# The spread stage of a graph kernel: edge pairs loaded two steps ahead into two buffers per quarter

## The reference

```python
# layer 0: attention over edges
out_i = softplus(concat(x[i], edge_attr) @ W).reshape(-1, 4, 64)
out_j = softplus(concat(x[j], edge_attr) @ W).reshape(-1, 4, 64)
alpha = softplus((concat(out_i, out_j) * att).sum(-1))      # then batch norm, softplus, segment softmax
x = layernorm(x + segment_sum(out_j * alpha, i).mean(heads) + bias)
# layer 1: two graph convolutions with symmetric norm and self loops
h = D @ (A + I) @ D @ (x @ W1) + b1                         # D = deg ** -0.5, A[d, s] = number of edges s -> d
h = D @ (A + I) @ D @ (h @ W2) + b2
x = layernorm(x + relu(h))
```

## Time and profile before

| | us |
|---|---|
| median of 3 runs | 6508.17 |
| the runs | 6492.07 to 6529.35 |
| the profiled execution, its own time | 6569.77 |
| its span, first to last instruction | 6568.1 |
| mean granted TensorE clock, share of full | 0.876 |

### The profile page before, as it was taken

How to read it: one execution, slowest core, us unless ns; L and a number is a source line. 1 busy time by engine, 2 the same in 40 slices (tenths; PEclk the granted TensorE clock), 3 DMA queues, 4 the chain that set the end, 5 groups by cost and what they waited for, 6 DMA issues and landing times. The chain is left out here.

```text
span 6568.1 us, 161934 instructions
## 1 busy us (share of the span) xinstructions
PE 4909.4 (75%) x32887; PEld 3154.3 (48%) x32888; DVE 4742.2 (72%) x21938; ACT 4010.7 (61%) x10577; POOL 3842.7 (59%) x5381
## 2 busy tenths in 40 slices
PE   1466676776767666674999999999948888886699
PEld 0234444444444344442555555555525556554699
DVE  6566666666666666664999999999986767777333
ACT  4344555555555555554999999989967777776100
POOL 1366666666666666565666666666637777776000
PEclk8577777777778888777999999999979999998799
DMA  8755555555555455555444444444417777775698
GB/s 227 232 180 180 188 188 182 186 185 186 189 174 179 167 172 178 168 177 153 104 103 104 103 105 105 103 103 104 103 40 218 216 216 224 215 212 176 247 360 345
DMA packets 1161941, 1148.62 MB, mean 175 GB/s; under 512 B 516532, under 2 KB 1023523, under 8 KB 1142980
## 3 DMA queue, kind: packets, MB, share of 16 engines
q1 hardware_dynamic: 1033656, 743.67, 40.2%
q0 software_dynamic: 88560, 319.28, 13.0%
q10 hardware_dynamic: 39580, 84.01, 3.4%
HBM read 716.98 MB, written 429.60 MB: 175 GB/s over the span
## 5 line engine op out<-in xcount | busy, mean ns | idle before, releaser
L914 POOL DMA_INDIRECT rows<-rowS,idx x1616 | 1732.5, 1072 | 1006.7 <-issue 469.7
L1185 PE MATMUL psa<-one_c,one_s 128*128 128x392 bf16 x2352 | 641.3, 393 | 654.8 <-DVE one_s L996 414.9
L2425 PE MATMUL psm<-msg,onem 128*128 128x260 f32 x3648 | 915.8, 394 | 212.7 <-issue 180.5
L988 DVE TENSOR_TENSOR one_c<-ioc,pairS 128x1176 bf16<-128x1176 f16 x784 | 599.4, 765 | 603.8 <-remote 340.4
L1699 DVE CUSTOM_DVE_ANT_1 junk<-bufh,attb 128x128 bf16<-128x128 f32 x3648 | 973.7, 301 | 0.0
L2346 POOL TENSOR_TENSOR msg<-oj,heads 128x512 f32<-128x512 f32 x760 | 796.9, 1072 | 215.3 <-DMA oj<-rows 179.0
L2425 PEld LDWEIGHTS psm<-msg,onem 128*128 128x128 f32 x3648 | 649.9, 190 | 478.2 <-issue 402.0
L1078 ACT ACTIVATE lgS<-preS 128x1024 f32<-128x1024 f32 x404 | 413.2, 1023 | 729.6 <-remote 375.4
L1659 POOL TENSOR_SCALAR one<-io128b,side 128x128 bf16<-128x128 bf16 x912 | 738.9, 810 | 63.5 <-DMA side<-rows 40.1
L1782 PE MATMUL pre<-P3h,oneT 128*128 x5472 | 757.0, 275 | 0.0
L1694 DVE CUSTOM_DVE_ANT_0 junk<-bufh,attb 128x64 bf16<-128x64 f32 x3648 | 742.1, 238 | 10.2 <-ACT bufh L1742 6.4
(11 more groups left out here) (306 smaller groups left out, 9238.3 us busy)
## 6 DMA issues: line engine op xcount, KB each, us to landing
oj<-rows SPq DMA_DIRECT2D x912, 256.0 KB
bufh<-rows SPq DMA_DIRECT2D x912, 128.0 KB, 2.5
adj<-adj SPq DMA_DIRECT2D x70, 1568.0 KB, 9.9
adj<-cnts ACTq DMA_DIRECT2D x49, 1568.0 KB
side<-rows SPq DMA_DIRECT2D x912, 68.0 KB, 2.3
eaS<-in_edge_attr_dram SPq DMA_DIRECT2D x201, 256.0 KB
low<-dlow SPq DMA_DIRECT2D x202, 252.0 KB
adj_early<-adj SPq DMA_DIRECT2D x28, 1568.0 KB, 8.4
```

Of the source, the lines that this page charges most:

```text
L914: eng.indirect_dma_start(out=m["rows"][h], out_offset=bass.IndirectOffsetOnAxis(ap=idx[s][:, k:k + 1], axis=0), in_=rows[s][:, k, :], in_o ...
L988: eng.tensor_tensor(one_c[r][:, :, :].rearrange("p k (a w) -> p k a w", w=WIDE), m["ioc"][:, q, None, :].rearrange("p k (a w) -> p k a w", ...
L1185: mm = eng.matmul(psa[r][:, 0:z.GC], one_s[r][:, k, :], one_c[r][:, k, :], start=(k == 0), stop=(k == GT - 1))
L2425: mm = eng.matmul(psm[j][:, 0:C + H], one[q][:, k, :], msg[q][:, k, :], start=(k == 0), stop=(k == UT - 1))
```

## The change

Each quarter gets two pair buffers, chosen by s % 2, with a semaphore each. SP loads the pairs of step t+2 where it loaded those of step t+1, and ahead of the loop it loads the pairs of steps 0 and 1. The wait before a load asks for `lanes` of step t as before, since the buffer that step t+2 takes is the one that step t used. `columns` counts the landings of its buffer by `turns(b, s)`, which is 2b + s // 2.

```diff
-        pair = [sb(ctx, f"pairS{q}", [P, GT, 2, WIDE], fp16) for q in range(GQ)]
+        pair = [[sb(ctx, f"pairS{q}{j}", [P, GT, 2, WIDE], fp16) for j in range(2)] for q in range(GQ)]
...
-        pair_in, cols_made, built, copied = ([sem(ctx, f"{n}{q}") for q in range(GQ)] for n in (
-            "pair_in", "cols_made", "built", "copied"))
+        cols_made, built, copied = ([sem(ctx, f"{n}{q}") for q in range(GQ)] for n in ("cols_made", "built", "copied"))
+        pair_in = [[sem(ctx, f"pair_in{q}{j}") for j in range(2)] for q in range(GQ)]
...
             def load_pairs(b, s, q):
                 t = step(b, s)
                 e = eng.value_load(m["startS"][0:1, span(t * GQ + q, 1)], min_val=0, max_val=NG * P * K)
-                wait(eng, cols_made[q], t)
-                eng.dma_start(pair[q][:, :, :, :].rearrange("p k n w -> p (k n w)"),
+                wait(eng, cols_made[q], t - 1)
+                eng.dma_start(pair[q][s % 2][:, :, :, :].rearrange("p k n w -> p (k n w)"),
                               m["pairs"][bass.ds(e, GT * P), :].rearrange("(p k) c -> p (k c)", k=GT))\
-                   .then_inc(pair_in[q], 16)
+                   .then_inc(pair_in[q][s % 2], 16)
 
             def body(b, s):
-                near, two = later(b, s, 1), later(b, s, 2)
+                two = later(b, s, 2)
                 if exists(*two):
                     load_ea(*two)
                     load_low(*two)
-                more = dense(near[0])
+                more = dense(two[0])
                 if more:
-                    load_pairs(*near, 0)
-                    load_pairs(*near, 1)
+                    load_pairs(*two, 0)
+                    load_pairs(*two, 1)
                 if exists(*two):
                     load_window(*two)
                 if more:
-                    load_pairs(*near, 2)
-                    load_pairs(*near, 3)
+                    load_pairs(*two, 2)
+                    load_pairs(*two, 3)
...
-            for q in range(GQ):
-                load_pairs(0, 0, q)
+            for s in range(2):
+                for q in range(GQ):
+                    load_pairs(0, s, q)
...
-                eng.wait_ge(pair_in[q], (t + 1) * 16)
+                eng.wait_ge(pair_in[q][s % 2], (turns(b, s) + 1) * 16)
```

More of the change, by code:

```diff
@@ L989, in columns @@
                                   m["ioc"][:, q, None, :].rearrange("p k (a w) -> p k a w", w=WIDE).to_broadcast(shape),
-                                  pair[q][:, :, 1, None, :].to_broadcast(shape), ALU.is_equal)
+                                  pair[q][s % 2][:, :, 1, None, :].to_broadcast(shape), ALU.is_equal)
             def lanes(b, s, q):
@@ L997, in lanes @@
                                   m["io128b"][:, None, :].rearrange("p k (a w) -> p k a w", w=WIDE).to_broadcast(shape),
-                                  pair[q][:, :, 0, None, :].to_broadcast(shape), ALU.is_equal).then_inc(cols_made[q], 1)
+                                  pair[q][s % 2][:, :, 0, None, :].to_broadcast(shape), ALU.is_equal).then_inc(cols_made[q], 1)
             def adj(b, s, q):
```

## The result

The changed kernel took 6549.37 us in the median of 4 runs (6542.57 to 6556.0), the kernel before 6501.04 us in the median of its 4 (6492.07 to 6529.35). The ratio is 1.006, with a 95% interval of 1.0036 to 1.0084. I had forecast 6493 us, in a range of 6448 to 6522: the change costs time where I had it gain a little. Two later comparisons on other chips gave 1.0049 [1.0032, 1.0067] and 1.0032 [1.0019, 1.0044]. The ratios are those on record, with their intervals; they are not the quotients of the medians printed beside them, from which they differ by up to 0.0016.

What follows compares the result with a forecast made beforehand. It found no engine full and took the stage as a chain of waits between engines that each run in order. The terms summed to −15 us, from the 6508 us median to 6493 us, range 6448 to 6522.

Steps and rivals of the forecast that it cites:

- The pair waits go: DVE before `columns`: waits for pairs, 88.4 us over the stage, fall to under 10 us.
- SP's lateness stays: SP at the block's end: q = 0 pairs still issued 2 to 3 us behind `load_ea`, eleven behind the last pairs.
- The cover that I had named: Stage start: four more pair loads delay `load_ea` by at most 4.3 us, hidden because DVE needs the low part later.
- Buffers, semaphores and the wait value cost nothing: Four more buffers and semaphores, and DVE's register work for the new wait value: cost 0.
- My slower rival: DVE's pair waits: computing each wait value costs 1.5 us per block, 74 us in all, giving 6567 us; chance 0.10.
- `psr` is late next: DVE's wait for PE's rank counts grows from 2.5 toward 3.8 us per block, leaving a gain of 15 us.
- the 6 us of the comparison: Stage halves with and without fills: 25 blocks with fills would gain 0.25 us each, 6 us.
- the 28 us of the single block: PE in one block: `adj` of q = 0 could start at most 1.4 us earlier, 28 us for 20 waits.
- the wait for `psr` took everything: Rival at DVE's wait for rank counts: it takes the whole gain, 6508 us, no change; chance 0.22.
- The comparison of the two halves: Stage blocks: 53.75 us each with fills, 53.50 us later with few pair waits, so pair waits do not set the pace.
- my forecast for this view: Block stores: every 53.0 to 53.6 us in the first half, still every 53.5 us in the second.
- The unnamed waits were pairs too: Rival before `columns`: the 340.4 us of "remote" waits also go, some 343 us gained in all, 6165 us; chance 0.02.

Runs made afterwards that it cites:

- buffers_only: Changed kernel with two buffers and semaphores per quarter and the new wait count, but all pairs loaded one step ahead; 6553.54 us, 0.9986 of the kernel before.
- after_again: The changed kernel timed once more, unedited, against the kernel before on the same chip; 6590.73 us, ratio 1.0049.
- after_third: The changed kernel timed a third time, unedited, against the kernel before on another chip; 6587.60 us, ratio 1.0032.
- q0_only: Changed kernel with only quarter 0 loaded two steps ahead, quarters 1 to 3 one step ahead; 6582.51 us, 1.0035 of the kernel before.
- the first question: Whether buffers and semaphores or the loads cost time: copies of both kernels and two partial versions, timed on a chip where the kernel before took 6557.84 us.
- gate_after2: Changed kernel, POOL's half 0 scatters at s = 0 held until PE made the next step's rank counts; 6559.12 us, 0.9994 of the kernel before.
- both exchanges: `add_up` of half 0 put ahead of the next step's `columns`: in the kernel before 6686.87 us, 1.0187; in the changed kernel 6697.06 us, 1.0193.
- gate_before2: Kernel before, with only the wait of POOL's half 0 scatters at s = 0 for PE's next rank counts; 6587.63 us, 1.0024 of the kernel before.
- the gate at s = 2: Changed kernel with the scatter gate at s = 2 instead of s = 0; 0.9971 and 0.9949 of the kernel before, both on 46-us chips.
- the gate together with the early `add_up`, addup_gate_before: Kernel before with `add_up` of half 0 ahead of `columns` and the scatter gate at s = 0; 6137.43 us, 0.9926, on a 46-us chip.
- the 1.9%: Loss from putting `add_up` of half 0 ahead of `columns` on a 54-us chip; 1.0187 in the kernel before, 1.0193 in the changed kernel.
- gate_after: Changed kernel, POOL's half 0 scatters at s = 0 held until PE made the next step's rank counts; 6146.62 us, 0.9953, on a 46-us chip.
- gate_before: Kernel before, with only the wait of POOL's half 0 scatters at s = 0 for PE's next rank counts; 6178.62 us, 0.9988, on a 46-us chip.
- the exchange alone: Kernel before with `add_up` of half 0 ahead of the next step's `columns`; 0.9932 on a 46-us chip, 1.0187 on a 54-us chip.
- before_again: The kernel before, unedited, timed against itself; 6556.47 us, ratio 0.9996.
- addup_first_after: Changed kernel with `add_up` of half 0 ahead of the next step's `columns`; 6697.06 us, 1.0193 of the kernel before.

## Why the prediction was wrong

**The pair waits go: right.** They fall from 80.3 to 1.8 us in the stretch of the earlier trace rows. For the whole stage I had said under 10.

**SP's lateness stays: right.** Over the 25 places behind a block's fills the first pair load follows `load_ea` by 3.6 us in the mean and the last pair load by 9.1 us (3.2 and 10.0 before). One of them:

```profile
1043.81 2.86 SPq L1445 DMA_DIRECT2D rows<-fill  x2
1047.29 0.36 SPq L844 DMA_DIRECT2D eaS<-in_edge_attr_dram  x1
...
1050.50 2.16 SPq L864 DMA_DIRECT2D pairS<-pairs  x2
```

At the stage's start `load_ea` of step 2 goes out at 300.78 us, 5.66 us later than before. The first pair load was already 0.58 us later (291.42 against 290.84), so the four more loads took 5.1 us where I had allowed 4.3. The cover that I had named holds all the same, for DVE has no wait before its use of step 2's low part at 308.61. SP's queue there and DVE's timeline:

```profile
300.78 0.37 SPq L844 DMA_DIRECT2D eaS<-in_edge_attr_dram  x1
```

```profile
308.12 0.57 DVE L940 TENSOR_TENSOR ohr<-io,hi_src 128x400 bf16<-128x400 bf16 x1
308.61 0.48 DVE L950 TENSOR_SCALAR ohT<-low,wsc 126x1024 bf16<-126x1024 bf16 x1
```

**Buffers, semaphores and the wait value cost nothing: right,** by 0.9986 for buffers_only. The instructions in question even fell, from 225 of 45 to 50 ns to

```profile
L985 DVEq FUSED_REGOPS  x45: 57/57/65, 342.6 to 2820.9; - x45
```

My slower rival, with its chance of 0.10, had the right sign for the wrong reason; nothing of its mechanism is there.

**`psr` is late next: right in the place, wrong in size and sign.** The term was "between the 6 us of the comparison and the 28 us of the single block", a gain of 15 us. The wait before L968 in the first half grew from 2.5 to 4.8 us per block (101.7 us over 21 blocks), where I had expected 3.8. The runs show not a gain but a loss, 20 to 40 us by the ratios. The step that failed is the one under the term: I took the time at which PE's counts are ready as given, so that the worst that could happen on this path was that the wait for `psr` took everything and the change gave nothing. I said what SP's queue would do and what DVE would wait for next, and did not ask what DVE releases earlier. It is `add_up` of half 0, and behind it the scatters on POOL. The waits of POOL showed it before the change: 246.5 us of waiting for DVE's `add_up`, the largest of its named waits in the stage. In its place the runs showed that with the new loads the scatters at s = 0 start 1.7 us earlier and the counts for s = 1 are ready 0.8 us later, and that a gate on these scatters brings the ratio from 1.0032 to 0.9994.

**The comparison of the two halves** showed that blocks without pair waits were no shorter, and that was a sound warning; but it compares two halves of one kernel and could not show a loss. The stores of the changed kernel, as the earlier trace rows:

```profile
L1112 ACTq DMA_DIRECT2D adj<-cnts x22: 338/338/361, 510.6 to 1631.6; - x22
...
L1112 ACTq DMA_DIRECT2D adj<-cnts x24: 338/339/365, 1688.9 to 2921.2; - x24
```

That is 1121.0 / 21 = 53.4 us and 1232.3 / 23 = 53.6 us, against 53.75 and 53.50. It is inside my forecast for this view, and it misled: in after_again, after_third and q0_only a block takes 54.5, 54.8 and 54.8 us over the whole stage. One profile of each kernel can't carry a difference of half a microsecond a block.

**The unnamed waits were pairs too: refuted** on 54-us chips, "remote" before `columns` stays at 361.2 against 340.4 us. The rule of the Trainium skill that the prediction weighed there ("Perfetto Trace Analysis", Optimization Strategy: a repeating gap can mean too few buffers) says what can be; for the pair buffers these runs do not bear it out: they were added and the gap kept 493.9 of its 603.8 us. Other buffers were not tried.

What stays open: by what way the early scatters make the count late, and how that costs a block its time. The trace shows PE's own rows over early and its consumers waiting. Timeline of the changed kernel in one bad block, PE, then DVE, then POOL:

```profile
728.92 0.81 PE L1157 MATMUL psr<-ohr,onesb 128*128 128x400 bf16 x5
730.09 0.29 PE L1157 MATMUL psr<-ohr,onesb 128*128 128x150 bf16 x3 [0.36 <-issue]
...
734.49 2.66 PE L1169 MATMUL preS<-W2d,eaT 64*128 64x256 f32 x5 [0.84 <-issue]
```

```profile
731.61 0.16 DVE L966 COPY rowS<-ends 128x16 f32 x1
738.97 0.57 DVE L968 TENSOR_TENSOR ranks<-psr,base 128x400 f32<-128x400 f32 x1 [7.20 <-remote]
```

```profile
731.36 0.96 POOL L915 DMA_INDIRECT rows<-rowS,idx  x1 [0.30 <-issue]
...
736.42 0.96 POOL L915 DMA_INDIRECT rows<-rowS,idx  x1 [0.30 <-issue]
740.21 0.95 POOL L915 DMA_INDIRECT rows<-rowS,idx  x1 [2.83 <-PE preS L1175]
```

The last rank matmul ends at 730.38 by the record, and DVE may go on only at 738.97, while POOL sends one scatter after another. ACT, which waits for the `adj` matmuls behind them (the last recorded to end at 732.82), goes on at 739.02 too, after 7.61 us without work. Whether the scatters' transfers, POOL's own work for them or something between PE and its supply of instructions is what meets, no run tells.

There is a rival that no run tests. The granted clock goes with the loss: on the chip of the first question the runs of the kernel before have a mean of 0.881, those of after_again 0.878 and of q0_only 0.879; on the chip of after_third it is 0.881 for before, 0.878 for after_third, 0.883 for gate_after2 and 0.873 for both exchanges. Among the runs of the kernel before on these two chips 0.001 less clock goes with 2 to 4 us more time, only loosely, so 0.003 would be 6 to 12 us of the loss (an estimate). Whether the clock falls because PE stands idle in other places, or the loss comes in part through the clock, stays open; gate_before2 loses at a clock of 0.881 against 0.880.

Nor was it tried whether leaving these scatters out does the same as delaying them, and on a 54-us chip neither the gate at s = 2 nor the gate together with the early `add_up` was timed. So that the place in front of the long count matters, and that the 1.9% is the same effect, is argued and not shown.

Of the new versions timed on both kinds of chip (gate_after, gate_before and the exchange alone) gate_after is the best compromise: 0.9994 on a 54-us chip and 0.9953 on a 46-us one. addup_gate_before is 0.9926 on the latter.

## What to carry to other kernels

Before taking a wait away, list what the waiting engine releases right behind it, not only what it waits for next. In this kernel a wait seems to have done the work of a schedule; where that may be so, try an explicit gate in its place, and test the two together, since here each alone lost. An effect under 1% is judged on many runs on one chip, never on two profiles.

## What the hardware showed unexpectedly

The same kernel took 6173.16 to 6177.84 us (medians) on three chips and 6501.04 to 6569.91 us on others, 5 to 6% apart. The granted clock of the profiles is 0.908 to 0.917 on the first and 0.871 to 0.884 on the second. The order of edits by time is not the same on the two: `add_up` first is 0.9932 on one and 1.0187 on the other. On the first POOL has next to no time to spare (2244 of 2260 us above), and the wait before ranks is 0.0 to 0.1 us in all nine profiles; on the second that wait is 136.0 (before_again) to 380.1 us, the latter in addup_first_after (290 to 2985 us):

```profile
L968 DVE TENSOR_TENSOR ranks<-psr,base 128x400 f32<-128x400 f32 x193 | 110.1, 571 | 380.1 <-remote 236.6 <-PE psr L1157 140.9 <-issue 2.5
```
